# Sixteen-head attention: two head groups weighed at a time, keys, maxima and division in other slots

## The reference

```python
q = (query @ wq.T + bq).reshape(B, Tq, HEADS, HEAD_DIM).transpose(0, 2, 1, 3)
k = (key @ wk.T + bk).reshape(B, Tk, HEADS, HEAD_DIM).transpose(0, 2, 1, 3)
v = (value @ wv.T + bv).reshape(B, Tk, HEADS, HEAD_DIM).transpose(0, 2, 1, 3)
scores = jnp.einsum('bhqd,bhkd->bhqk', q, k) * scale
scores = jnp.clip(scores, -100.0, 100.0)
scores = jnp.where(mask == 0, -jnp.inf, scores)
attn = jax.nn.softmax(scores, axis=-1)
out = jnp.einsum('bhqk,bhkd->bhqd', attn, v)
out = out.transpose(0, 2, 1, 3).reshape(B, Tq, HEADS * HEAD_DIM)
return out @ wo.T + bo
```

## Time and profile before

| | us |
|---|---|
| median of 3 runs | 1678.51 (1676.42 to 1682.44) |
| the profiled execution | 1674.06 |
| its span in the trace | 1672.2 |
| TensorE busy in the span | 1412.8 (84%) |
| VectorE busy | 1187.5 (71%) |
| ScalarE busy | 695.2 (42%) |
| GpSimd busy | 346.3 (21%) |

### The profile page before, as it was taken

How to read it: one execution, slowest core, us unless ns; L and a number is a source line. 1 busy time by engine, 2 the same in 40 slices (tenths; PEclk the granted TensorE clock), 3 DMA queues, 4 the chain that set the end, 5 groups by cost and what they waited for, 6 DMA issues and landing times. The chain is left out here.

```text
span 1672.2 us, 39863 instructions
## 1 busy us (share of the span) xinstructions
PE 1412.8 (84%) x12076; PEld 1018.0 (61%) x12076; DVE 1187.5 (71%) x4000; ACT 695.2 (42%) x1643; POOL 346.3 (21%) x482
## 2 busy tenths in 40 slices
PE   1899999699588888888699769999978998968887
PEld 1677777466356666665355447777757887845554
DVE  6576766578568888888578746666655885669995
ACT  2466666433234444444333326565652224321111
POOL 1223232144222222222134313232310000000000
PEclk9799999899889999999799879999998999989998
DMA  3544433100132222222000043323315422300000
GB/s 107 157 101 100 101 95 87 48 30 0 25 79 69 63 65 68 67 66 46 25 2 0 18 136 74 80 69 81 74 27 176 150 95 88 106 18 9 11 11 14
DMA packets 175974, 110.24 MB, mean 66 GB/s; under 512 B 80810, under 2 KB 172973, under 8 KB 175277
## 3 DMA queue, kind: packets, MB, share of 16 engines
q1 hardware_dynamic: 175900, 109.32, 24.9%
HBM read 83.47 MB, written 25.77 MB: 65 GB/s over the span
## 5 line engine op out<-in xcount | busy, mean ns | idle before, releaser
L628 ACT ACTIVATE p<-ps 125x448 f32<-125x448 f32 x576 | 311.8, 544 | 250.7 <-PE ps L914 131.4
L769 DVE TENSOR_REDUCE negm<-ps 112x1 f32<-112x375 f32 x512 | 258.6, 542 | 70.5 <-PE ps L886 69.1
L886 PE MATMUL ps<-kst,qst 96*112 96x375 f16 x768 | 236.1, 345 | 55.4 <-DVE negm L769 24.6
L901 PE MATMUL ps<-qst,kst 112*125 112x224 f16 (+1 forms) x1152 | 209.9, 264 | 4.7 <-POOL qst L603 3.2
L603 POOL TENSOR_TENSOR qst<-m_row,diag 16x448 f16<-16x448 f16 x128 | 128.2, 1029 | 322.2 <-ACT m_row L674 322.2
L1267 PE MATMUL ps<-fw,xs_e 128*112 128x512 f16 x768 | 188.0, 385 | 0.0
L901 PEld LDWEIGHTS ps<-qst,kst 112*125 112x125 f16 (+1 forms) x1152 | 145.3, 137 | 46.1 <-ACT p L628 12.4
L886 PEld LDWEIGHTS ps<-kst,qst 96*112 96x112 f16 x768 | 97.6, 132 | 101.8 <-DVE negm L769 48.2
L925 PE MATMUL ps<-p,v 125*32 125x112 f32 x4608 | 150.8, 264 | 1.2 <-ACT p L628 1.0
L765 DVE CUSTOM_DVE_ANT_0 with_mask<-ps,mask_add 112x375 f16<-112x375 f32 x256 | 135.4, 546 | 19.0 <-issue 17.3
L816 PE MATMUL ps<-ctxT,wkv_split 128*128 (+1 forms) x576 | 118.4, 346 | 34.4 <-DVE ctxT L786 32.5
(11 more groups left out here) (227 smaller groups left out, 2345.3 us busy)
## 6 DMA issues: line engine op xcount, KB each, us to landing
kst<-k_split SPq DMA_DIRECT2D x288, 93.8 KB, 2.4
k_split<-ks SPq DMA_DIRECT2D x48, 375.0 KB, 3.7
fw<-in_w SPq DMA_DIRECT2D x16, 1024.0 KB, 6.7
qst<-q_split SPq DMA_DIRECT2D x576, 14.0 KB, 1.8
stage<-in_ctxT SPq DMA_DIRECT2D x16, 375.0 KB, 3.8
ctxn<-in_ctx SPq DMA_DIRECT2D x16, 375.0 KB
q_split<-qs SPq DMA_DIRECT2D x48, 112.0 KB, 2.1
fw<-in_ew SPq DMA_DIRECT2D x2, 2048.0 KB, 7.6
```

Source lines behind the costliest of these rows:

```text
L628: act.activation(g.p[hg % 2][:, kt, :], ps[0:KR, BK_ST + s % 2, 0:4 * S], ACT.Exp).then_inc(s_exp, 1)
L769: dve.tensor_reduce(g.negm[1 - par][:, h:h + 1], scored, AX_X, ALU.max, negate=True).then_inc(s_max, 1)
L886: mm = pe.matmul(ps[0:S, BK_S + h % 2, 0:SK], g.q_stack[q][0:96, h, :], g.k_stack[q][0:96, h // 2, :], start=True, stop=True)
L901: mm = pe.matmul(bank[:, 2 * r * S:2 * (r + 1) * S], g.k_stack[par][0:rows, pr, kt * KR:(kt + 1) * KR], g.q_stack[par][0:rows, 2 * pr:2 * ...
```

## The change

- `weigh` takes a pair of head groups: 24 matmuls in one go in two slots of a batch (7 and 13 in layers 0 and 2, 8 and 14 in layer 1) instead of 12 in each of four (3, 7, 11, 13; in layer 1 4, 7, 10, 13).
- `g.p` has a third buffer, in a part of the weights' buffer `fw` that is free during attention. Head groups 0 to 3 use buffers 0, 1, 2, 0. ScalarE waits for the weighing ahead of group 0 and of group 3.
- In layers 0 and 2 the scores stand in other slots: none in front of slot 1, two in slots 1, 3 and 9, and one each in 2, 4 to 8 and 10 to 13. The second half of the keys moves from slot 2 to slot 3.
- In both plans `back` moves from slot 6 to 7, and VectorE's division stands behind the maxima of its slot instead of ahead of them.

```diff
--- before.py
+++ after.py
@@ -21,6 +21,8 @@
 KT = 3
 KR = SK // KT
 HG = 4
+HG_PAIRS = HG // 2
+P_OF = (0, 1, 2, 0)
 PAIRS = H // 2
 E = 8
 F = 1024
@@ -344,6 +346,7 @@
     g.m_stack = [sb(f"mst{i}", [128, H, S], F16) for i in range(2)]
     g.v = [sb(f"v{i}", [KR, KT, H, 32], F32) for i in range(2)]
     g.p = [sb(f"p{i}", [KR, KT, 4 * S], F32) for i in range(2)]
+    g.p.append(g.fw[1][0:KR, 2048:2048 + KT * 4 * S].rearrange("p (t c) -> p t c", t=KT))
     g.negm = [sb(f"negm{i}", [S, H], F32) for i in range(2)]
     g.maxima = [sb(f"maxima{i}", [S, 2 * H], F32) for i in range(2)]
     g.m_row = [sb(f"m_row{i}", [128, S], F16) for i in range(2)]
@@ -390,17 +393,17 @@
     def __init__(self, scores, values, weigh, turn, back, out, stats, q, maxima, split, rows, keys):
         self.scores = spread(scores)
         self.values = {s: kt for kt, s in enumerate(values)}
-        self.weigh = {s: hg for hg, s in enumerate(weigh)}
+        self.weigh = {s: pair for pair, s in enumerate(weigh)}
         self.turn, self.back, self.out, self.q, self.maxima, self.split = turn, back, out, q, maxima, split
         self.stats = {s: part for part, s in enumerate(stats)}
         self.rows, self.keys = rows, {s: m for m, s in enumerate(keys)}
 
 
 PLANS = {
-    False: Plan(scores=[1, 1, 2, 3, 4, 4, 5, 5, 6, 7, 8, 8, 9, 9, 10, 12], values=[10, 13, 14], weigh=[3, 7, 11, 13],
-                turn=4, back=6, out=9, stats=[9, 10, 11], q=2, maxima=14, split=12, rows=1, keys=[0, 2]),
-    True: Plan(scores=[0, 1, 2, 3, 4, 5, 5, 6, 6, 7, 8, 8, 9, 10, 10, 11], values=[8, 10, 12], weigh=[4, 7, 10, 13],
-               turn=5, back=6, out=9, stats=[9, 10, 11], q=3, maxima=13, split=12, rows=0, keys=[1, 2]),
+    False: Plan(scores=[1, 1, 2, 3, 3, 4, 5, 6, 7, 8, 9, 9, 10, 11, 12, 13], values=[10, 13, 14], weigh=[7, 13],
+                turn=4, back=7, out=9, stats=[9, 10, 11], q=2, maxima=14, split=12, rows=1, keys=[0, 3]),
+    True: Plan(scores=[0, 1, 2, 3, 4, 5, 5, 6, 6, 7, 8, 8, 9, 10, 10, 11], values=[8, 10, 12], weigh=[8, 14],
+               turn=5, back=7, out=9, stats=[9, 10, 11], q=3, maxima=13, split=12, rows=0, keys=[1, 2]),
 }
 ST_SLOTS = HG * KT
 STACK_DMAS = 3 + 6
@@ -622,10 +625,12 @@
                 idx = i * ST_SLOTS + s
                 hg, kt = s // KT, s % KT
                 act.wait_ge(s_st, idx + 1)
-                if kt == 0:
-
-                    at_least(act, s_pv, i * HG + hg - 1)
-                act.activation(g.p[hg % 2][:, kt, :], ps[0:KR, BK_ST + s % 2, 0:4 * S], ACT.Exp).then_inc(s_exp, 1)
+                if kt == 0 and hg == 0:
+
+                    at_least(act, s_pv, i * HG_PAIRS)
+                if kt == 0 and hg == 3:
+                    at_least(act, s_pv, i * HG_PAIRS + 1)
+                act.activation(g.p[P_OF[hg]][:, kt, :], ps[0:KR, BK_ST + s % 2, 0:4 * S], ACT.Exp).then_inc(s_exp, 1)
 
             def body(turn, on):
                 i, par = turn.i, turn.u
@@ -679,12 +684,12 @@
                         act.wait_ge(s_v, KT * (i + 1) + kt + 1)
                         if kt == 0:
 
-                            at_least(act, s_pv, i * HG)
+                            at_least(act, s_pv, i * HG_PAIRS)
                         act.activation(g.v[q][:, kt, :, 0:HD],
                                        ps[0:KR, BK_KV + (kt + 1) % 2, 0:D].rearrange("p (h d) -> p h d", h=H),
                                        ACT.Copy).then_inc(s_vsb, 1)
                 if on["e"]:
-                    act.wait_ge(s_pv, (i + 1) * HG)
+                    act.wait_ge(s_pv, (i + 1) * HG_PAIRS)
 
                     at_least(act, s_ot, i)
                     act.activation(g.pv[:, :], pv[:, 0:4 * S], ACT.Copy).then_inc(s_pvsb, 1)
@@ -749,8 +754,6 @@
                         dve.wait_ge(s_raw, i * ST_SLOTS + s + 1)
                         st = ps[0:KR, BK_ST + s % 2, 0:4 * S]
                         dve.tensor_scalar(st, st, -CLIP, CLIP, ALU.max, ALU.min).then_inc(s_clip, 1)
-                    if on["o"] and s == plan.turn:
-                        divide(i - 1)
                     if on["m"]:
                         for h in plan.scores.get(s, []):
                             dve.wait_ge(s_s, (i + 1) * H + h + 1)
@@ -768,6 +771,8 @@
                             else:
                                 dve.tensor_reduce(g.negm[1 - par][:, h:h + 1], scored, AX_X, ALU.max,
                                                   negate=True).then_inc(s_max, 1)
+                    if on["o"] and s == plan.turn:
+                        divide(i - 1)
                     if clipped and on["m"] and s == max(plan.scores):
                         largest = g.maxima[1 - par][:, H:2 * H]
                         dve.wait_ge(s_max, (i + 2) * H)
@@ -914,16 +919,18 @@
                 pe.matmul(bank, g.mask_add[par][:, kt * KR:(kt + 1) * KR], g.m_stack[par][:, 4 * hg:4 * hg + 4, :],
                           start=False, stop=True, skip_group_check=True).then_inc(s_st, 1)
 
-            def weigh(i, par, hg):
-                pe.wait_ge(s_exp, i * ST_SLOTS + (hg + 1) * KT)
-                if hg == 0:
+            def weigh(i, par, pair):
+                pe.wait_ge(s_exp, i * ST_SLOTS + 2 * (pair + 1) * KT)
+                if pair == 0:
                     pe.wait_ge(s_vsb, KT * (i + 1))
 
                     at_least(pe, s_pvsb, i)
-                for kt in range(KT):
-                    for j in range(4):
-                        mm = pe.matmul(pv[32 * j:32 * j + 32, hg * S:(hg + 1) * S], g.v[par][:, kt, 4 * hg + j, :],
-                                       g.p[hg % 2][:, kt, j * S:(j + 1) * S], start=(kt == 0), stop=(kt == KT - 1))
+                for hg in (2 * pair, 2 * pair + 1):
+                    for kt in range(KT):
+                        for j in range(4):
+                            mm = pe.matmul(pv[32 * j:32 * j + 32, hg * S:(hg + 1) * S],
+                                           g.v[par][:, kt, 4 * hg + j, :], g.p[P_OF[hg]][:, kt, j * S:(j + 1) * S],
+                                           start=(kt == 0), stop=(kt == KT - 1))
                 mm.then_inc(s_pv, 1)
 
             def body(turn, on):
```

## The result

The changed kernel takes 1759.44 us (median of 4 runs, 1758.85 to 1763.44), the kernel before 1678.55 (1676.42 to 1682.44): ratio 1.0487, 95% interval 1.0465 to 1.0509. I had forecast 1732, in a range from 1700 to 1758, with 0.85 on slower. The sign was right; the loss is 81 us and not 54, and the time lies 1.4 us above the range.

The account below looks back on a forecast made before the run. TensorE was taken to bound layers 0 and 2, VectorE's clipping to pace layer 1. Losses of 28 and 27 us gave +55 on 1674.06, so 1729, with 1732 given as median; range 1700 to 1758.

Parts of the forecast that it names:

- rival 3: In the merged pair, the second group saves nothing (0.81 instead of 0.54): +26 more, 1758; chance 4 in 100.
- The 0.74 saved: Layers 0 and 2: two merged pairs save 0.54 a batch, taken as 0.74 with fewer entries and exits.
- The walk through slots 3 to 7 and slot 12: Layers 0 and 2: new TensorE waits for VectorE's maxima, 1.61 in slots 3 to 7 and 1.05 in slot 12.
- Rival 1: Faster: the slot 5 wait goes, saving 1.25 + 0.54 a batch in layers 0 and 2, 1621; chance 9 in 100.
- +0.93 per batch: Layers 0 and 2: sum a batch, 0.26 + 1.61 + 1.05 of waits less 1.25 and 0.74.
- the stretch from the last values to the second keys: Layers 0 and 2: slot 2's scoresT piece loses the keys ahead and waits 0.26 for the first exp.
- the context's split: Layer 0: one VectorE operation that comes ahead of head 15, priced at 0.1.
- 1 us for its last two batches: Layers 0 and 2: an estimated loss of 0.5 for each of the last two batches, which project no keys.
- +1.38 for the pair of slot 8: Layer 1: the pair delays a `shift_and_mask` that waited for nothing, by 1.35 to 1.38 a batch.
- The 0.54 at the end, less 0.14: Layer 1: the last weighing becomes 0.54 longer; 0.14 is what waits at a batch's end swallow.
- the division: Layer 1: the division moves by 1 us in VectorE's own queue and costs nothing.
- rival 4: The clock falls: some 3 us of matmuls doubled in each batch of layers 0 and 2, +90, 1820; chance 4.

Follow-up runs that it names:

- experiment 1: Kernel before with merged weighing pairs and the third buffer alone, in all three layers; scores, keys and division as before: 1716.46 against 1677.99, 1.0219.
- experiment 8: Kernel before with the merged weighing pairs in layers 0 and 2 alone, everything else as before: 1670.5 against 1678.79, 0.9942.
- experiment 2: Kernel before with the new slots of scores and keys, back in slot 7 and division behind the maxima, four weighings kept: 1703.97 against 1677.99, 1.0141.
- experiment 10: Experiment 3's kernel with the weighings of slots 3 and 11 made as well in layers 0 and 2: 1735.01 against 1678.68 for the kernel before, 1.0321.
- experiment 9: Experiment 3's kernel with the second keys left in slot 2: 1699.09 against 1678.68 for the kernel before, 1.0119.
- experiment 3: Whole change in layers 0 and 2; layer 1 keeps four weighings and back in slot 6, with division behind the maxima: 1727.03 against 1677.99 before, 1.0282.
- experiment 11: Whole change, with groups 0 to 2 weighed once more at the old slots in layer 1: 1749.64 against 1678.68 for the kernel before, 1.0414.
- experiment 6: Kernel before with only layer 1 changed, groups 0 and 1 paired in slot 8: 1712.81 against 1678.79, 1.0197.
- experiment 7: Kernel before with only layer 1 changed, groups 2 and 3 paired in slot 14: 1682.44 against 1678.79, 1.0018.
- experiment 4: Kernel before with the division behind the maxima and back in slot 7 alone, in all layers: 1687.41 against 1677.99, 1.0053.
- experiment 5: Experiment 1's kernel with groups 0 to 2 weighed once more at the old slots in layer 1: 1696.45 against 1678.79 for the kernel before, 1.0099.

## Why the prediction was right, and where it wasn't

The span grew by 84.8 and I had 55. Of the 29.8 that are missing, 15.1 lie in layer 1 (42.4 against 27.3) and 14.6 in layers 0 and 2 (42.6 against 28).

- **Merging, layers 0 and 2.** The pair was priced nearly right (48 records in 1.36, forecast 1.32), so rival 3 is out. The 0.74 saved was too much. In steps from start to start, averaged over eight batches of layer 2, the four weighings with what they add to the matmuls ahead and behind hold TensorE for 3.41, the two pairs for 2.86: 0.55 saved. It was also wrong as a term by itself. In layer 2 and layer 0 the pairs alone save 0.2 and 0.35 (experiments 1, 8), the slots alone cost 0.35 and 0.94 (experiment 2), and both together cost 1.19 and 1.33. The removed weighings had stood in waits, as forecast; experiment 10 puts them back for 0.03 in layer 2.
- **The walk through slots 3 to 7 and slot 12** holds to 0.02 where a row can be compared (2.29, 2.89, 1.04). The keys' slot was shown to be worth 0.69 by experiment 9. Rival 1 fell for the reason given against it: VectorE had neither head 3's nor head 12's maximum in time.
- **+0.93 per batch was too little:** 1.19 in layer 2, 1.33 in layer 0. The same steps give the places of the missing 0.26 in layer 2: 0.19 is the saving (0.55 for 0.74), 0.11 the stretch from the last values to the second keys (0.37 longer than before, forecast 0.26), and the waits of slots 3 to 7 and 12 are 0.05 below the forecast. That is read from the rows, not tested. In layer 0 the context's split, priced at 0.1, is larger in experiment 2 (0.47); in the whole change the maxima's transpose starts only 0.05 later than in layer 2. There the first keys start up to 1.13 after the last values do (0.82 at most before) and the piece of slot 2 0.42 to 0.51 after the score ahead (0.30 in layer 2). How much of that is the split isn't told apart.
- **The edges were mis-sized.** I gave a layer 1 us for its last two batches. In layer 2 the last four periods cost 4.6 more than before, against 2.9 (2 x 0.93 + 1). With the same plan of that layer they cost 3.2 more in experiment 3, at a clock of 1.00, and 6.0 in experiment 11, at 0.94; in the change it is 0.97. So the clock is in this term too. Layer 0 loses another 4.5 ahead of its first transpose (87.34 against 82.86). The keys' slot goes with it: in the five kernels with keys in slot 3 that transpose comes at 87.3 to 90.2, in the nine with slot 2 at 82.1 to 85.9; kernels with the same layer 0 differ by up to 3.2. I hadn't looked at a layer's first batch.
- **Layer 1's terms held at the full clock:** +1.38 for the pair of slot 8 was 1.41 alone (experiment 6), and a batch at the full clock takes 23.53, forecast 23.51. The 0.54 at the end, less 0.14, was 0.26 (experiment 7), and the division cost 0.15 (experiment 4), which I had at nothing; the two errors nearly cancel. Over the 15 periods the layer without falls costs 344.1 - 314.7 = 29.4.
- **The step that failed is rival 4**, the fall of the clock: the sum of layer 1 had nothing for it, and the rival had it in the wrong place and at a chance of 4. I looked for the fall in layers 0 and 2, where the clock stays at 1.00 in full batches, and argued from a wait of 0.92 in one go that was harmless. No run shows the 3 us of matmuls doubled in each batch that its 1820 takes; in full batches the clock falls in layer 1 alone, where a period then takes 25.0 (at 0.93) or 26.6 (at 0.87) instead of 23.5. In layer 1 it costs 354.6 - 344.1 = 10.5 in the trace and 9.8 by the medians. Of the 10.5, 8.2 lie in the first 12 periods, where the falls come and go with the extra matmuls, and 2.3 in the last three, where the clock also differs between executions of one plan (the last four periods of layer 1 take 75.3 in the kernel before, at 0.95, and 80.5 in experiment 8, which has the same plan there, at 0.86). That it is the clock, and not something else in the plan, is shown by experiments 5 and 11: more matmuls in the same waits, nothing removed, and the long batches are gone from the first 12 periods; in the stretch shown the lost time is in longer matmuls. Single gaps don't tell the two apart: in layer 1 the clock goes from 0.96 to 0.54 after gaps of 0.80 and 0.54, and in the full batches of layers 0 and 2 it stays at 1.00 with gaps of up to 0.88.

Without the falls the change takes 1749.6 (experiment 11), at the upper end of my own forecast's range. So the other misses (about 19 us of the span, in the batches of layers 0 and 2, the layers' edges and layer 1's full-clock batches) would not by themselves have left the range. What in the pattern of work makes the clock fall in one period and not in the next stays open, and so does why the extra matmuls give back 14.3 in layer 1 beside experiment 1 but 10.5 beside the change.

## What to carry to other kernels

Before taking work away from an engine, ask in which wait it stands: work inside a wait is nearly free (0.03 us for 24 matmuls here), and two edits that each open or fill the same waits can't be priced one at a time (in layer 2 -0.2 and +0.35 apart, +1.19 together). Where TensorE is paced by another engine, small matmuls between waits may be what holds its clock (layer 1 of the change at 0.94, with the extra matmuls at 0.99), so look at the stretch's clock and not at the length of single gaps. And walk through a layer's first and last batches too, since here they held 1.7 us more than priced in layer 2 and 4.5 ahead of layer 0's first transpose.

## What was not expected of the hardware

- TensorE's granted clock fell to about half (0.54 over the stretch shown, 0.50 from 611.55 to 614.90) in 5 of layer 1's first 12 periods, though TensorE is nowhere idle for more than 0.83 at a time between 535 and 840; with 72 more records a batch it fell in none of them. A period at 0.93 takes 25.0 instead of 23.5, the one at 0.87 26.6.
- 24 extra float32 matmuls on 32 columns cost 0.03 us a batch in layer 2, where TensorE waited anyway (17.72 to 17.75), and 0.2 in layer 0 (17.8 to 18.0).
- A merged pair costs about what the rate inside a group says: 48 records in 1.36, against 0.78 for 24, so 0.58 for 24 more, where the rate gave 0.54.
